# The opening of a two-layer LSTM kernel: gathers in fours, head products and a layer 1 matrix ahead of the first cell, a shorter band, POI rows for 128 rows at a time

## What is computed

```python
rp = concat([region_tbl[region_idx], poi_tbl[poi_idx]], -1)          # 8 + 4 features
nv = concat([rp @ W_rp + b_rp, coords @ W_co + b_co], -1)            # 32 + 8
conv = elu(conv1d(nv, conv_w, width 3, 'VALID') + conv_b)            # 8 steps of 32
emb = tanh(concat([car_tbl[car_idx], week_tbl[week_idx], time_tbl[time_idx]], -1))   # 27
x = concat([conv, broadcast(emb)], -1)
h = lstm(x, Wih0, Whh0, bih0, bhh0)        # H = 256, 1024 gate columns
h = lstm(h, Wih1, Whh1, bih1, bhh1)
return ((h[:, -1] @ W1 + b1) @ W2 + b2) @ W3 + b3                    # 512 columns
```

## Time and profile before

| what | us |
|---|---|
| median of 3 runs | 1119.18 (1118.47 to 1119.56) |
| the profiled execution | 1118.79 |
| its span | 1117.0 |
| TensorE busy | 1076.6 (96%) |
| VectorE, ScalarE, GpSimd busy | 743.0, 510.1, 319.9 |
| start of `cell(second)` on TensorE | 102.10 |

### The profile page before, as it was taken

One profiled execution on the slowest core, in us unless ns is written; L12 is line 12 of the kernel. 1 busy time (PEld: TensorE's weight loads), 2 busy tenths in 40 slices (PEclk: granted clock), 3 DMA queues, 4 the chain that ended last, 5 costly groups with the idle time before them and its releaser, 6 DMA issues.

```text
span 1117.0 us, 14516 instructions
## 1 busy us (share of the span) xinstructions
PE 1076.6 (96%) x4994; PEld 520.8 (47%) x4994; DVE 743.0 (67%) x1136; ACT 510.1 (46%) x735; POOL 319.9 (29%) x338
## 2 busy tenths in 40 slices
PE   5959999999999999999999999999999999999998
PEld 4835444444444544444444544444444544444444
DVE  1558858576676767666686768666676758666653
ACT  1334544444455544444455544444455545444432
POOL 6550025562540015562541015552442000000000
PEclk9779999999999999999999999999999999999999
DMA  9510001000010101000010101000010100000001
GB/s 224 144 17 15 1 2 30 3 2 1 2 31 1 40 2 31 3 2 1 2 30 2 40 1 29 5 2 1 2 30 1 38 1 21 9 0 1 0 1 38
DMA packets 34382, 22.59 MB, mean 20 GB/s; under 512 B 22922, under 2 KB 27018, under 8 KB 34186
## 3 DMA queue, kind: packets, MB, share of 16 engines
q1 hardware_dynamic: 21648, 20.54, 6.7%
q0 software_dynamic: 9984, 1.12, 2.6%
q10 hardware_dynamic: 2682, 0.04, 0.2%
HBM read 11.18 MB, written 4.19 MB: 14 GB/s over the span
## 4 chain that ended last, share of the span: by engine, by line
PE 93%; DVE 3%; issue 1%; DMA 1%; ACT 1%; SPq 1%; ACTq 0%; DVEq 0%
PE acc L1224 52%; PE acc L1215 28%; PE acc L1206 5%; PE acc L1069 2%; PE aux L1314 2%; PE acc L1139 1%; DMA w<-in_L_rec_W 1%; PE aux L1174 1%; SPq L413 1%; PE aux L1304 1%; ACT gates L683 1%; PE aux L1130 0%; PE aux L1098 0%; PE aux L1084 0%; DVE gates L925 0%
## 5 line engine op out<-in xcount | busy, mean ns | idle before, releaser
L1224 PE MATMUL acc<-h_part,wh 128*128 128x512 f16 (+1 forms) x2688 | 656.1, 380 | 1.6 <-DVE h_part L976 1.6
L1224 PEld LDWEIGHTS acc<-h_part,wh 128*128 128x128 f16 x2688 | 245.2, 98 | 322.0 <-issue 55.7
L1215 PE MATMUL acc<-h_part,wh 128*128 128x512 f16 (+1 forms) x1488 | 358.9, 379 | 0.4 <-issue 0.3
L683 ACT ACTIVATE gates<-acc,gate_bias,unscale 128x512 f32<-128x512 f32 x254 | 196.1, 777 | 328.9 <-PE acc L1224 278.0
L683 ACT ACTIVATE gates<-gates,gate_bias,unscale 128x512 f32<-128x512 f32 x242 | 190.2, 811 | 150.1 <-DVE gates L925 143.8
L1215 PEld LDWEIGHTS acc<-h_part,wh 128*128 128x128 f16 x1488 | 144.4, 98 | 178.2 <-issue 7.6
L527 POOL DMA_INDIRECT feat<-in_L_rec_region_tbl,region_idx x160 | 160.4, 1002 | 163.7 <-PE acc L1224 124.7
L925 DVE TENSOR_TENSOR gates<-acc,emb_gates 128x512 f32<-128x512 f32 x242 | 161.6, 686 | 54.9 <-PE acc L1224 46.3
L527 POOL DMA_INDIRECT feat<-in_L_rec_poi_tbl,poi_idx x120 | 121.7, 1014 | 114.5 <-PE acc L1224 96.9
L1206 PE MATMUL acc<-x_in,wx 96*128 96x512 f32 (+1 forms) x248 | 139.2, 567 | 15.7 <-DMA x_in<-conv_hi 11.9
L972 DVE TENSOR_TENSOR h_full<-gates,tanh_c 128x512 f32<-128x512 f32 x120 | 82.6, 688 | 75.8 <-ACT tanh_c L688 69.6
(11 more groups left out here) (126 smaller groups left out, 375.4 us busy)
## 6 DMA issues: line engine op xcount, KB each, us to landing
out<-y SPq DMA_DIRECT2D x16, 256.0 KB, 2.6
x_in<-conv_hi SPq DMA_DIRECT2D x56, 64.0 KB
feat<-in_L_rec_region_tbl,region_idx POOLq DMA_INDIRECT x160
w<-in_L_rec_W SPq DMA_DIRECT2D x2, 1024.0 KB
w_nat<-in_L_rec_Whh SPq DMA_DIRECT2D x2, 1024.0 KB, 13.1
w<-in_L_rec_W SPq DMA_DIRECT2D x1, 2048.0 KB
feat<-in_L_rec_poi_tbl,poi_idx POOLq DMA_INDIRECT x120
x_in<-conv_lo SPq DMA_DIRECT2D x28, 64.0 KB
```

Of the source, the lines that this page charges most:

```text
L683: nc.scalar.activation(gates[layer][:, j, g, :], source, ACT.Tanh if g == GATE_G else ACT.Sigmoid, bias=gate_bias[:, layer, m:m + 1], scal ...
L1215: mm = nc.tensor.matmul(bank, wh[:, 1, a, c, rows], h_part[0][:, s.write_slot, b, c, :], start=(c == 0 and a == b == HI), stop=(s.first an ...
L1224: mm = nc.tensor.matmul(bank, wh[:, own_w, a, c, rows], h_part[layer][:, s.read_slot, b, c, :], start=False, stop=(c == HK - 1 and a == LO))
```

## The change

All of it concerns the opening, and the order of rows.

- Row b of a batch is now partition b % 128, group b // 128. Indices, coordinates and output follow. The first batch's region indices and coordinates are loaded by themselves, the other batches' late.
- Car, time and week indices are loaded as 16 rows of 128 each, turned by one TensorE transpose (`turn_small`) and copied out of `acc`'s fourth bank; the second product of W12 waits for that.
- The load order of SyncE: the three small index loads and all of W2 come ahead of the POI indices, W3 ahead of the biases, Wih1 and Whh1.
- The 16 gathers of the first steps are issued in fours, each four waiting for its rows; the 8 of the embeddings too.
- W_rp and W_co are loaded as they lie, three times into one block matrix, and transposed by TensorE (`turn_proj`); `band` is four products of 120 rows, and one for the bias.
- `poi_rows` makes 40 products of 128 rows by 24 columns with a block-diagonal POI table, in place of 80.
- `product_head(0)`, `product_head(1)` and `turn_wh(1)` stand ahead of `cell(first)`; layer 1's diagonal is made by eight ScalarE activations. Three of the four quarters of `turn_wh(0)` stand ahead of `turn_steps`.
- `cell(first)` waits for the first step's six copies alone (`x0_put`), `cell(second)` for the next six.
- b12 is summed by one VectorE addition (`w12_t` gets a 257th column), the head sum is made in two halves.

```diff
-        PAIR_DMAS = 3 * PAIR * 2
+        HALVES_DMAS = 3 * 2
...
+                put = x_put[1] if s else (x_put[0], x_second_put)[k]
                 for half in range(2):
                     row = (half * PAIR + k) * D_CONV
                     put_x(eng, s * PAIR + k, slice(row, row + D_CONV), slice(s * HALF, (s + 1) * HALF),
-                          slice(half * HALF, (half + 1) * HALF), x_put[s])
+                          slice(half * HALF, (half + 1) * HALF), put)
...
+            load(idx_raw["region"][:, 0:GR, :], rows_of("r_region_idx", 0, GR), first_idx_in)
+            sp.wait_ge(small_zeroed, 1)
+            for k, at in (("car", CAR_AT), ("time", TIME_AT), ("week", DAY_AT)):
+                load(small_raw[at:at + NB * GR, :], d[f"r_{k}_idx"].rearrange("(g p) -> g p", p=P), small_idx_in)
             load(w1_nat[:, :, :], d["W1"].rearrange("(a p) n -> p a n", p=P), w1_in)
             w2_rows = d["W2"].rearrange("(k p) n -> p k n", p=P)
-            load(w2[:, :, 0:D2 // 2], w2_rows[:, :, 0:D2 // 2], w2_in[0])
-            for k in ("car", "time", "week"):
-                load(idx_raw[k][:, :, 0].rearrange("p (n g) -> p n g", g=GR),
-                     d[f"r_{k}_idx"].rearrange("(n p g) -> p n g", p=P, g=GR), idx_in[k])
+            for half in range(2):
+                cols = slice(half * (D2 // 2), (half + 1) * (D2 // 2))
+                load(w2[:, :, cols], w2_rows[:, :, cols], w2_in[half])
...
+            load(w3[:, :, :], d["W3"].rearrange("(k p) n -> p k n", p=P), w3_in)
             for layer in range(2):
                 for i, k in enumerate(("bih", "bhh")):
                     load(bias_in[:, layer, i, :], d[f"{k}{layer}"].rearrange("(m p) -> p m", p=P), bias_loaded)
-            load(w3[:, :, :], d["W3"].rearrange("(k p) n -> p k n", p=P), w3_in)
-            load(w_nat[2][:, :, :], d["Whh1"].rearrange("(m p) k -> p m k", p=P), w_in[2])
+            for i, k in ((1, "Wih1"), (2, "Whh1")):
+                load(w_nat[i][:, :, :], d[k].rearrange("(m p) k -> p m k", p=P), w_in[i])
             load(b3_row[:, :], d["b3"].rearrange("(a n) -> a n", a=1).partition_broadcast(P)[:, 0, :], b3_in)
-            load_rows("poi")
+            load(idx_raw["region"][:, GR:NB * GR, :], rows_of("r_region_idx", GR, NB * GR), later_idx_in)
+            load(idx_raw["poi"][:, GR:NB * GR, :], rows_of("r_poi_idx", GR, NB * GR), later_idx_in)
+            load(coords[:, GR:NB * GR, :], coord_rows[:, GR:NB * GR, :], later_coords_in)
...
-            out_rows = d["out"].rearrange("(n p g) o -> p n g o", p=P, g=GR)
+            out_rows = d["out"].rearrange("(n g p) o -> p n g o", p=P, g=GR)
...
+                    for t in range(PAIR_WIN):
+                        gather_steps(t, t + 1, False, rows_first_in)
+                        pool.wait_ge(rows_first_in, (t + 1) * GR * DMA)
                     pool.wait_ge(coords_in, DMA)
                     copy_coords()
-                    pool.wait_ge(rows_first_in, GR * PAIR_WIN * DMA)
-                    pool.wait_ge(idx_ready, 3)
-                    gather_emb()
+                    pool.wait_ge(small_put, 1)
+                    for g in range(0, GR, 2):
+                        gather_emb(g, g + 2)
+                        pool.wait_ge(emb_rows_in, (g + 2) * (2 * DMA))
...
+            act.wait_ge(proj_zeroed, 2)
+            for k in range(TAPS):
+                row, col = k * D_FEAT, k * D_NV
+                load(proj_nat[row:row + D_REG + D_POI, col:col + D_RP], d["W_rp"], proj_in)
+                load(proj_nat[row + D_REG + D_POI:row + D_FEAT, col + D_RP:col + D_NV], d["W_co"], proj_in)
...
+            def put_proj():
+                act.wait_ge(proj_turned, 1)
+                act.wait_ge(proj_t_zeroed, 1)
+                nc.scalar.copy(proj_t[:, PAD:PAD + TAPS * D_FEAT], aux[0:TAPS * D_NV, 1, 0:TAPS * D_FEAT]
+                               ).then_inc(proj_put, 1)
+                nc.scalar.copy(proj_bias[:, :], aux[0:TAPS * D_NV + 1, 1, BIAS_AT:BIAS_AT + 1]).then_inc(proj_put, 1)
+
+            def diagonal1():
+                act.wait_ge(prep, 9)
+                for m in range(M):
+                    nc.scalar.activation(diag[1][:, m, :], ident[:, :], ACT.Copy, scale=row_scale[:, 1, m:m + 1]
+                                         ).then_inc(diag_ready[1], 1)
...
+            put_wh_hi(0, 0, 3)
             put_turned(feat_t[0:KP, 0, :], aux[0:KP, 0, :], first_turned, 1, first_turned_put)
-            put_wh_hi(0, 0, 1)
+            put_wh_hi(0, 3, 4)
             elu_parts(0, slice(0, HALF))
-            put_wh_hi(0, 1, 4)
-            emb_tanhs(0, acc[:, 3, :])
-            act.wait_ge(prep, 4)
+            put_head_hi(0)
+            diagonal1()
+            put_head_hi(1)
+            emb_tanhs(0, acc[:, 0, :])
+            put_wh_hi(1)
             act.wait_ge(bias_ready, 1)
             first, second = opening_cells(STEPS)
             cell_acts(first)
-            put_emb_gates(0, 0)
-            put_head_hi(0)
-            put_emb_gates(0, 1)
+            for part in range(3):
+                put_emb_gates(0, part)
+            put_wh_hi(2)
             put_turned(feat_t[0:KP, 1, :], acc[0:KP, 0, :], turned[0], 1, turned_put[0])
-            put_head_hi(1)
             elu_parts(1, slice(0, HALF))
-            put_emb_gates(0, 2)
-            put_wh_hi(1)
-            put_wh_hi(2)
             cell_acts(second)
...
+            indices(0, "region", REG, slice(0, GR), (first_idx_in, DMA))
+            small_indices()
             put_band()
+            put_conv_bias()
+            poi_parts()
             poi_one_hot()
-            poi_parts()
             row_maxima(0)
             row_scales(0)
-            put_conv_bias()
+            week_lookup()
             put_poi()
             put_wx_lo()
-            row_maxima(1)
+            add_head_bias()
+            put_wh_lo(0)
             dve.wait_ge(bias_loaded, 4 * DMA)
             nc.vector.tensor_tensor(gate_bias[:, :, :], bias_in[:, :, 0, :], bias_in[:, :, 1, :],
                                     ALU.add).then_inc(bias_ready, 1)
-            put_wh_lo(0, 0, 1)
             elu(0, slice(0, HALF), (0, slice(0, HALF)), ())
-            put_wh_lo(0, 1, 4)
+            sum_head_bias(0, K2 // 2)
+            put_head_lo(0)
+            row_maxima(1)
+            row_maxima(2)
+            row_scales(1)
+            put_head_lo(1)
             split_emb(0)
+            put_wh_lo(1)
             first, second = opening_cells(STEPS)
             cell(first)
-            row_maxima(2)
-            row_scales(1)
-            sum_head_bias()
-            put_head_lo(0)
-            put_head_lo(1)
+            sum_head_bias(K2 // 2, K2)
+            put_wh_lo(2)
             elu(1, slice(0, HALF), (0, slice(HALF, NCOL)), ())
-            put_wh_lo(1)
-            put_wh_lo(2)
             dve.wait_ge(head_bias_acc, 1)
             dve.wait_ge(b3_in, DMA)
             nc.vector.tensor_tensor(b_head[:, :], acc[:, 1, :], b3_row[:, :], ALU.add).then_inc(head_bias_put, 1)
             cell(second)
-            indices(4, "poi", POI)
+            dve.wait_ge(x_second_put, HALVES_DMAS * DMA)
+            later = slice(GR, NB * GR)
+            indices(1, "region", REG, later, (later_idx_in, 2 * DMA))
+            dve.wait_ge(idx_ready, 2)
+            indices(2, "poi", POI, later, (later_idx_in, 2 * DMA))
...
             def band():
-                pe.wait_ge(proj_in, 3 * DMA)
+
+                pe.wait_ge(proj_put, 2)
+                pe.wait_ge(conv_w_in, 2 * DMA)
                 for s in range(TT):
-                    for k in range(TAPS):
-                        at = PAD - (s + k) * D_FEAT
-                        mm = nc.tensor.matmul(aux[0:KF, 0, s * D_CONV:(s + 1) * D_CONV], proj_t[:, at:at + KF],
-                                              conv_w[:, k, :], start=(k == 0), stop=(k == TAPS - 1))
+                    at = PAD - s * D_FEAT
+                    mm = nc.tensor.matmul(aux[0:KF, 0, s * D_CONV:(s + 1) * D_CONV], proj_t[:, at:at + KF],
+                                          conv_w[0:TAPS * D_NV, s, :], start=True, stop=True)
                 mm.then_inc(band_acc, 1)
-
-            def product_conv_bias():
-                pe.wait_ge(conv_bias_in, (2 + TT) * DMA)
-                for s in range(TT):
-                    for k in range(TAPS):
-                        mm = nc.tensor.matmul(aux[s * D_CONV:(s + 1) * D_CONV, 1, 0:1], conv_w[:, k, :],
-                                              proj_bias[:, :], start=(k == 0), stop=(k == TAPS - 1))
-                mm.then_inc(conv_bias_acc, 1)
+                nc.tensor.matmul(aux[:, 1, P:P + 1], conv_w[:, :, :].rearrange("k s o -> k (s o)"), proj_bias[:, :],
+                                 start=True, stop=True).then_inc(conv_bias_acc, 1)
...
             def poi_rows():
-                pe.wait_ge(poi_part_put, 3)
+                pe.wait_ge(poi_block_put, SIDES)
                 pe.wait_ge(poi_hot_put, 1)
```

(64 more changed lines are left out.)

236 lines of the change are left out of this document (141 added, 95 removed).

## The result

| what | before | after |
|---|---|---|
| median on the chip of the prediction | 1119.37 (1118.47 to 1119.59) | 1106.42 (1103.19 to 1108.00) |
| ratio | | 0.9876 [0.9864, 0.9889] |
| profiled execution | 1118.79 | 1107.28 |
| span | 1117.0 | 1105.5 |
| start of `cell(second)` | 102.10 | 88.13 |

The kernel is 13 us faster, 4.4 less than the forecast of 1102.0 had it. `cell(second)` starts 14.0 us earlier (forecast: 19.2), and the block behind it is 2.5 longer (forecast: 2.1). 14.0 - 2.5 = 11.5 is the difference of the two profiled executions.

What follows compares the result with a forecast made beforehand. TensorE, without gaps behind the opening, bounds the kernel, so only time before cell(second) can be gained: 1118.79 - 19.2 + 2.1 = 1101.7 us profiled, 1102 as median, range 1096 to 1110.

Steps and rivals of the forecast that it cites:

- The frame: Whole kernel: everything behind cell(second)'s start only moves, so time is 1118.79 us minus its earlier start plus any bubble.
- Part 1: Kernel start: W1 and W2's first half come some 1.3 us later; first product at 12.3 instead of 11.04 us.
- Part 2: W12, band, POI: W12 ends at 29.4 us, POI takes 4.0 plus 1.0 for holes, TensorE stands at 35.0 us.
- Part 4: Gathers in waited fours, the decisive term: 9.6 us a four, rows in at 43.2 us, 12.3 later than before.
- Rival (a): Gathers land as in quiet queues; TensorE's own 41.7 us decides instead of 43.2; 1099 us, chance 0.27.
- Rival (b): Gathers in fours still slower: 12 us a four gives 1111 us, 10.6 a four gives 1106; chance 0.22.
- Part 5: Up to cell(first): head products fill the hole, 2 us diagonal wait, turn_wh(1) 3.8 us; start 65.9, not 69.8 us.
- part 3: Turning Wih0 and Whh0: 3.8 and 2.9 us at full clock, 2.9 more at half; TensorE ready for turn_steps at 41.7.
- Part 6: From cell(first) to cell(second): ScalarE's activations and embedding copies pace it; cell(second) at 82.9 instead of 102.1 us, 19.2 earlier.
- rival (c): More comes back: b_head holds cell(second)'s fourth tile 3.5 us and part 3 runs at half clock; 1105.5 us, chance 0.09.
- What is given back: Behind cell(second)'s start: b_head holds the fourth tile 1.4 us, late VectorE sums cost 0.7 more; together 2.1 us.

Runs made afterwards that it cites:

- e2: Kernel after with the band behind the fifth product of W12 instead of the second; 1106.75 us, ratio 0.9994 to the kernel before.
- e1: Kernel after with the first 16 gathers and 8 embedding gathers issued without waits between fours; 1101.29 us, ratio 0.9942 to the kernel before.
- a1: Kernel after run again without an edit, on another chip; 1106.05 us, ratio 0.9984 to the kernel before.
- c2: c1 plus unused products in four waits of TensorE: five ahead of turn_wx, e4's in the others; 1095.09 us, ratio 0.9892 to the kernel before.
- c1: Kernel after with the edits of e1, e2 (band behind W12's fourth product here) and e10 together; 1099.27 us, ratio 0.9919 to the kernel before.
- e4: Kernel after with unused products, two ahead of turn_wh(1), four and one between the embedding products; 1101.30 us, ratio 0.9935 to the kernel before.
- b1: Kernel before run again without an edit, on another chip than the prediction's; 1107.98 us, ratio 0.9999 to the kernel before.
- e6: Kernel before with one part alone, each of the first two cells waiting for its own six copies; 1103.97 us, ratio 0.9966 to the kernel before.
- e10: Kernel after with VectorE adding the head bias (b_head) ahead of elu(1); 1104.47 us, ratio 0.9972 to the kernel before.

## Why the prediction was right, and where it was off

**The frame held.** The block behind `cell(second)` moved as one piece, and the time was what the start of `cell(second)` gave plus a small bubble.

**Part 1** was too late by 2.6 us (9.70 us against 12.3): W1 and W2 did not come later. Nothing of it reached the end, because the next load took it.

**Part 2** had the POI products at 4.0 + 1.0 us; with the gap behind them they took 2.2 (34.60 to 36.77). The part counted 40 products, half of the old ones, and the kernel has 20, a quarter; at the old pace of 63 ns each they make 1.26 us, and the row has 1.28. So the term was wrong in its count, and its doubt about the cost of a product was not needed. What the part missed is `conv_w`'s load: the band stood 4.66 us for it, and a clock of 0.80 from 20 to 37 us followed. I had looked for a late load at `turn_proj` only. The eight products of W12 took 1.9 us more than counted, too. These errors nearly cancelled, which is luck: `turn_wx` began at 36.77 where 35.0 was forecast, and TensorE was ready for `turn_steps` at 43.2, not 41.7. e2 shows that this cost nothing while the rows were late.

**Part 4** was right in mechanism and nearly in size. Rows at 44.97 against 43.2, since the first four took 12.4 us, under the loads of W1 and W2, and not 9.6. By the rule of the Trainium skill that the prediction cites ("DMA: Bandwidth & Descriptors", section "Anatomy of one DMA — SWDGE (gpsimd) path", about 2.0 us for such a DMA) the rows would have been in near 29 us; the trace has 44.97. Rival (a) fell with it. Rival (b) has 1106 us for fours of 10.6 us, and the median is 1106.42, but only 1.8 us of the miss are the rows'; the rest is in parts 5 and 6, so that hit would be luck. What I did not ask is what the pacing was worth: e1 says that it costs 4.7 us, so issuing them all at once, as the kernel before does, would have been the better order.

**Part 5** is off by 3.0 us at `cell(first)`: 68.89 against 65.9. The rows are 1.8 of it (`turn_steps` at 45.32 against 43.5) and `turn_wh(1)` at 5.44 instead of 3.8 us is 1.6, less 0.4 over the other terms. The 2 us wait for layer 1's diagonal came as told, 1.95 us. The step that failed is the 3.8 us behind it: I gave grounds for full clock in part 3, for a stream without holes, and took it over to a place right behind a wait. In a1 these 3.8 us came out right (3.81), and the head products took 2.4 us more instead, behind a wait for the rows of 2.98 us in place of 2.09. So which of the two pays differs between executions of one kernel.

**Part 6** is off by another 2.2 us. The embedding products waited 4.10 and 0.80 us for ScalarE as the sum had it, but `turn_wh(2)` behind them took 6.09 us, 2.3 more. These two terms, 3.9 us, are the clock's: c2 takes both away, against c1, with work that means nothing, and e4 takes the second away. The forecast put half clock down only to the holes in front, in the earlier trace rows and in rival (c), and there at `turn_wx`. It should have priced its own new waits so. The Trainium skill, "TensorE: Matmul & The Clock Gate", section "What's actually happening", has the throttled state as the default that activity releases; the prediction cited it for the dense stretch, where the trace of after agrees (1.00 from 45 to 58 us), and not for the waits, where it bears just as much (0.83 from 69.8 to 100 us). In a1, behind the longer wait for the rows, the clock is 0.77 from 45 to 60 us.

**What is given back**, 2.1 us forecast, 2.5 measured, was right for a wrong reason in part. The wait for `b_head` is 0.84, not 1.4; the rest is in waits such as `x_in`'s, which a1 shows to vary.

**The step that the result can't speak for.** The sum took its start from an execution with holes that the traces of b1 and e6, on two other chips, don't show, and from a time that none of three other chips has. The change cuts these small products (24 to 5, 80 to 20), so a forecast of 17 us was near for that chip. Made on b1's rows, the same working has `cell(second)` at 82.9 against 92.13, 9.2 us, less the bubble of 2.1: 7. Of that, the 5.2 us go off that late rows and the clock cost in the profile of after, and some 2 stay; a1 measured 1.5. The measured 13 us is thus mostly the removal of what is added to the kernel before on the chip where it was timed, since the kernel after takes 1106.42 us there and 1106.05 on another. No run on that chip has the shorter band or POI rows alone. On the one other chip where both kernels ran, the change is worth 1.5 us (0.16%). The interval of that ratio, 0.9975 to 0.9992, lies just below 1, but the gain is less than the 0.2% taken as the limit of a measurement.

## What to carry to other kernels

A wait that TensorE is given in an opening can cost twice, its own length and the slower records behind it: price it so, or put work into it. Waits between indirect gathers are paid at the loaded latency of the queues, 10 us a four here; put them only where nothing waits for the rows. Count the products of a new loop from its bounds before pricing them. And when a profile shows gaps that wait for nothing, profile the same kernel on another chip before a change is credited with removing them.

## What the runs showed of the hardware

- The same kernel, without an edit, takes 1119.4 us on one chip and 1107.5 to 1108.1 on three others. In the two profiled executions compared, 9.4 us of it are in the first 52 us, in "issue" gaps among small products (3.8 and 2.7 us) and slower records beside them; what makes them is open.
- 32 records of 128x128 took 3.7 to 3.8 us at full clock and 5.44 to 6.09 behind idle stretches of 2 to 4 us in after; in a1 they took 3.81 behind a stretch of 2.15 us. With two unused products of about 0.9 us each in the first stretch and five in the second, they took 3.81 and 3.73 (c2, against 5.44 and 6.08 in c1).
- Behind a wait of 2.09 us for the rows, in after, the head products took 14.00 us; behind waits of 2.98 and 3.01 us, in a1 and e4, they took 16.4; behind 5.28 us, in e2, they took 14.00 again, and the small products between were the slow ones (8 records in 1.91 us in place of 1.06).
- 16 indirect gathers issued one behind the other from 4.67 us on were in at 31.3 us (e1), and in waited fours at 44.97 (after), with a DMA share of 0.9 to 1.1 up to 43 us.
- In the later batches, the longest of SyncE's pairs of `x_in` issues took 2.1 to 2.3 us in after, a1, e1, e10 and c1, and at most 1.5 us in b1 and before. How long TensorE then waited for `x_in` varied from 1.8 to 4.8 us between two executions of one kernel, after and a1.
